# Pairwise feature tower on one core: sums after every eight units, ScalarE copying two units of a run, transposes by halves of rows

## What is computed

```python
e = stack([tbl_f[ids[:, f]] for f in range(32)], axis=1)      # 1024 x 32 x 64
p, q = e[:, ROW], e[:, COL]                                   # 496 pairs
kp = einsum('bpj,ipj->bpi', p, kernel)
z = sum(kp * q, axis=-1)                                      # 1024 x 496
h = concatenate([z, dense_ctx], axis=1)                       # 512 columns
h = maximum(h @ W_top1 + b_top1, 0.0)                         # 512
h = maximum(h @ W_top2 + b_top2, 0.0)                         # 256
y = h @ W_top3                                                # 1024 x 1
```

## Time and profile before

| | |
|---|---|
| median of three executions | 438.9 us |
| the profiled execution | 438.72 us |
| its span | 436.9 us |
| TensorE busy | 429.6 us (98%) |
| VectorE busy | 300.4 us (69%) |
| GpSimd busy | 232.2 us (53%) |
| ScalarE busy | 70.9 us (16%) |
| products, 1984 instructions | 236.2 us |
| sums, 1984 instructions | 120.4 us |
| full transposes, 122 instructions | 26.9 us |

### The profile page before, as it was taken

How to read it: one execution, slowest core, us unless ns; L and a number is a source line. 1 busy time by engine, 2 the same in 40 slices (tenths; PEclk the granted TensorE clock), 3 DMA queues, 4 the chain that set the end, 5 groups by cost and what they waited for, 6 DMA issues and landing times.

```text
span 436.9 us, 10124 instructions
## 1 busy us (share of the span) xinstructions
PE 429.6 (98%) x4308; PEld 286.3 (66%) x4308; DVE 300.4 (69%) x300; ACT 70.9 (16%) x154; POOL 232.2 (53%) x249
## 2 busy tenths in 40 slices
PE   8969999999999999999999999999999999999997
PEld 6646666777677766676677766666667777754442
DVE  4746778877787777877877777887887778860000
ACT  1212110111121101012211110112111010101121
POOL 4777777777776666666466666664666600000000
PEclk9969999999999999999999999999999999999999
DMA  8543454441111111111111111111151100000000
GB/s 242 177 129 85 128 176 131 124 110 29 41 42 25 35 23 26 26 34 23 31 36 23 36 24 23 38 24 28 32 176 38 23 8 14 2 1 1 0 1 0
DMA packets 16513, 23.62 MB, mean 54 GB/s; under 512 B 5778, under 2 KB 9618, under 8 KB 16340
## 3 DMA queue, kind: packets, MB, share of 16 engines
q1 hardware_dynamic: 8080, 14.72, 10.9%
q0 software_dynamic: 7808, 8.01, 9.3%
q10 hardware_dynamic: 580, 0.23, 0.2%
HBM read 20.85 MB, written 0.00 MB: 48 GB/s over the span
## 4 chain that ended last, share of the span: by engine, by line
PE 97%; DMA 1%; POOL 1%; issue 0%; ACT 0%; POOLq 0%
PE kp L594 52%; PE z_ps L611 27%; PE kp L632 6%; PE tr_ps L578 5%; PE kp L638 3%; PE tr_ps L568 2%; PE kp L553 1%; DMA raw<-in_tbl,ids_sb 1%; PE z_ps L568 1%; POOL raw L421 1%; PE kp L645 0%; ACT prod L483 0%; POOL z_sb L411 0%; POOLq L724 0%
## 5 line engine op out<-in xcount | busy, mean ns | idle before, releaser
L531 DVE TENSOR_TENSOR prod<-kp,pair 128x1024 f32<-128x1024 f32 x224 | 260.1, 1217 | 83.4 <-PE kp L594 83.4
L421 POOL DMA_INDIRECT raw<-in_tbl,ids_sb x244 | 231.6, 949 | 117.9 <-issue 62.0
L594 PE MATMUL kp<-pair,k_sb 64*128 64x256 f32 x1984 | 236.2, 387 | 0.0
L594 PEld LDWEIGHTS kp<-pair,k_sb 64*128 64x128 f32 x1984 | 186.1, 188 | 35.7 <-DVE prod L531 6.8
L611 PE MATMUL z_ps<-prod,ones_sel 128*32 128x256 f32 x1984 | 120.4, 382 | 0.0
L611 PEld LDWEIGHTS z_ps<-prod,ones_sel 128*32 128x32 f32 x1984 | 57.9, 110 | 53.6 <-DVE prod L531 14.6
L439 ACT ACTIVATE pair<-tr_ps 128x256 f32<-128x256 f32 x63 | 24.3, 385 | 235.1 <-PE tr_ps L578 225.4
L578 PEld LDWEIGHTS tr_ps<-ident,raw 128*128 128x128 f32 x122 | 12.4, 141 | 27.8 <-issue 27.8
L541 DVE TENSOR_TENSOR prod<-kp,pair 128x512 f32<-128x512 f32 x48 | 30.0, 681 | 0.5 <-PE kp L594 0.5
L578 PE MATMUL tr_ps<-ident,raw 128*128 128x128 f32 x122 | 26.9, 302 | 3.4 <-DMA raw<-in_tbl,ids_sb 3.4
L632 PE MATMUL kp<-z_sb,k_sb 128*128 128x512 f32 x64 | 28.0, 595 | 0.0
(11 more groups left out here) (15 smaller groups left out, 20.2 us busy)
## 6 DMA issues: line engine op xcount, KB each, us to landing
k_sb<-in_kd SPq DMA_DIRECT2D x14, 512.0 KB, 3.8
raw<-in_tbl,ids_sb POOLq DMA_INDIRECT x244
pair<-pair SPq DMA_DIRECT2D x32, 64.0 KB
k_sb<-in_small SPq DMA_DIRECT2D x6, 256.0 KB, 6.6
k_sb<-in_w SPq DMA_DIRECT2D x1, 1024.0 KB
hot_ids_sb<-in_hot_ids SPq DMA_DIRECT2D x3, 256.0 KB, 6.2
k_sb<-in_kd SPq DMA_DIRECT2D x3, 256.0 KB, 2.9
z_sb<-in_dense SPq DMA_DIRECT2D x1, 512.0 KB, 3.6
```

What stands on the lines that cost most here:

```text
L421: nc.gpsimd.indirect_dma_start(raw[:, r % RAW_RING, i, n, :], None, tables[f], bass.IndirectOffsetOnAxis(ap=ids_sb[:, 2 * b + i, f:f + 1], ...
L531: nc.vector.tensor_tensor(prod[:, u % PROD_RING, :, :].rearrange("p q (i n) -> p (q i) n", i=UNIT_SLOTS), kp[u % KP_RING][:, :, :].rearran ...
L594: last = nc.tensor.matmul(kp[u % KP_RING][:, q, i * WIDTH:(i + 1) * WIDTH], k_sb[rows, x, :], pair[rows, group_place(st, owner // 2), :], ...
```

## The change

- Sums are made in batches of eight units from the second stage on (the last batch of a stage has six), and are issued after the seventh unit of the next batch. The first stage keeps batches of four. The run of products between two sums has so many units: seven, then fours, three; from unit 62 on seven, then eights, and sevens at the stage boundaries.
- `z_ps` is 128 x 2 x 256 and a sum takes 512 columns, both slots of a unit at once. The features' places in `z_sb`, the rows of W_top1 and the dense rows follow; the dense load is two planes, of 1 MB.
- In each run from unit 62 on, the units at places 1 and 3 (counted from 0) are copied by ScalarE from `kp` to `prod` (`spill`), and VectorE multiplies them in place in `prod` behind the other units of the run. `DONE_AT` gives each unit's place in VectorE's order. `prod` has 15 places.
- From group 6 of the second stage on an event carries two groups. An event whose unit follows sums is transposed by halves: each 128x128 block as two transposes of 64 rows against a 64x64 identity, into two banks of a `kp` buffer, and ScalarE copies them back in order. Other events keep the full form.
- `raw` has four places, and a gather waits for the event that read its place; the second group of a double event waits for six units more.

```diff
-KP_RING = 3
-PROD_RING = 12
-LAG = 3
-RAW_RING = 8
-RAW_LEAD = 5
+KP_RING = 3
+PROD_RING = 15
+RAW_RING = 4
-STAGES = (1, 1, 1, 1)
+STAGES = ((1,) * GROUPS, (1,) * 6 + (2,) * 5, (2,) * 8, (2,) * 8)
-BATCH_UNITS = (4, 4, 4, 4)
+BATCH_UNITS = (8,) * 4
+FIRST_BATCH_UNITS = (4,) * 8
+SPILL_AT = (1, 3)
+PACE = 6
-CHUNK_UNITS = CHUNK_TILES // (2 * UNIT_SLOTS)
+CHUNK_UNITS = P // 4
...
 def summed_behind(b):
     st, first, n = BATCHES[b + 1]
-    return first + min(LAG, n) - 1
+    return first + (n - 2 if n % 4 == 0 else n - 1)
+
+def spilled_units():
+    return [run[i] for run in runs()[1:-1] for i in SPILL_AT if i + KP_RING < len(run)]
+
+DVE_ORDER = [u for run in runs() for u in [u for u in run if u not in SPILLED] + [u for u in run if u in SPILLED]]
+DONE_AT = {u: i + 1 for i, u in enumerate(DVE_ORDER)}
+
+def done_through(n):
+    return max(DONE_AT[u] for u in range(n))
...
-TRANSPOSE_AT = [0, 0, 0, 1, 2, 4, 7, 10, 13, 16, 19, 23, 27, 31, 35, 39, 43, 47, 51, 55, 59, 61, 65, 69, 73, 77, 81,
-                85, 89, 93, 97, 101, 105, 109, 113, 117, 121, 123, 127, 131, 135, 139, 143, 147, 151, 155, 159, 163,
-                167, 171, 175, 179, 183, 185, 189, 193, 197, 201, 205, 209, 213, 217, 221, 225]
+TRANSPOSE_AT = [0, 0, 0, 1, 2, 4, 7, 10, 13, 16, 19, 23, 27, 31, 35, 39, 43, 47, 51, 55, 59, 62, 65, 69, 77, 85, 93,
+                101, 109, 117, 124, 131, 139, 147, 155, 163, 171, 179, 186, 193, 201, 209, 217]
...
+def gather_unit(r):
+    if r < RAW_RING:
+        return 0
+    e = EVENT_OF[r - RAW_RING]
+    st, k, n, raws = EVENT[e]
+    return TRANSPOSE_AT[e] + PACE if n == 2 and r - RAW_RING == raws[1] else 0
+
+def sums_before(u):
+    return u > 0 and BATCH_OF[u - 1] > 0 and u - 1 == summed_behind(BATCH_OF[u - 1] - 1)
+
+def by_halves(e):
+    return len(EVENT[e][3]) > 0 and sums_before(TRANSPOSE_AT[e])
+
+def home_unit(e):
+    return TRANSPOSE_AT[e] + EVENT[e][2]
...
 # gathers
-                if RELEASE[r]:
-                    pool.wait_ge(transposed, RELEASE[r] + 1)
+                if r >= RAW_RING and EVENT_OF[r - RAW_RING] != (EVENT_OF[r - RAW_RING - 1] if r > RAW_RING else None):
+                    pool.wait_ge(transposed, EVENT_OF[r - RAW_RING] + 1)
+                if gather_unit(r):
+                    pool.wait_ge(kp_done, gather_unit(r))
...
 # ScalarE, behind the evacuations and mixing copies of unit u
+            def spill(u):
+                act.wait_ge(reduced, BATCH_OF[u - PROD_RING] + 1)
+                act.wait_ge(kp_done, u + 1)
+                nc.scalar.activation(prod[:, u % PROD_RING, :, :], kp[u % KP_RING][:, :, :],
+                                     ACT.Copy).then_inc(spilled, 1)
...
 # VectorE
-            for u in range(UNITS):
+            for u in DVE_ORDER:
...
+                if u in SPILLED:
+                    dve.wait_ge(spilled, SPILLED.index(u) + 1)
+                    columns = prod[:, u % PROD_RING, :, :]
+                else:
+                    dve.wait_ge(kp_done, u + 1)
+                    columns = kp[u % KP_RING]
...
 # TensorE, transposes
+                if by_halves(e):
+                    pe.wait_ge(prod_done, DONE_AT[home_unit(e) - KP_RING])
...
+                        rows = raw[:, r % RAW_RING, i, :, :].rearrange("p a n -> p (a n)")
+                        if by_halves(e):
+                            to = ((g - k) * 2 + i) * 64
+                            for h in range(2):
+                                half = slice(64 * h, 64 * h + 64)
+                                last = nc.tensor.transpose(halves_ps(e)[:, h, to:to + 64], rows[half, :],
+                                                           ident[half, half])
...
 # TensorE, products
-                if u >= KP_RING:
-                    pe.wait_ge(prod_done, u - KP_RING + 1)
+                if u - KP_RING in SPILLED:
+                    pe.wait_ge(spilled, SPILLED.index(u - KP_RING) + 1)
+                elif u >= KP_RING:
+                    pe.wait_ge(prod_done, DONE_AT[u - KP_RING])
+                for e in range(len(EVENT)):
+                    if by_halves(e) and home_unit(e) == u:
+                        pe.wait_ge(evacuated, e + 1)
...
 # TensorE, sums
-                for t, u, i, q in tiles:
-                    g = t % 4
-                    col = 2 * ((t % CHUNK_TILES) // 4)
-                    last = nc.tensor.matmul(z_ps[32 * g:32 * g + 32, :], ones_sel[:, 30 - col:62 - col],
-                                            prod[:, u % PROD_RING, q, i * WIDTH:(i + 1) * WIDTH],
...
+                for v, u, q in tiles:
+                    j = v % CHUNK_UNITS
+                    g = 2 * (j % 2) + q
+                    col = 2 * (j // 2)
+                    last = nc.tensor.matmul(z_ps[32 * g:32 * g + 32, :, :].rearrange("p i n -> p (i n)"),
+                                            ones_sel[:, 30 - col:62 - col],
+                                            prod[:, u % PROD_RING, q, :],
```

More of the change, by code:

```diff
@@ L20 @@
 FC = (2 * TILES + DENSE) // P
-CHUNK_TILES = P // 2
+PAIRS = FC // 2
 N1, N2 = HID1 // P, HID2 // P
@@ L142, in batches @@
             first, end = c, min(c + CHUNK_UNITS, SLOTS // UNIT_SLOTS)
-            for n in BATCH_UNITS:
+            for n in BATCH_UNITS if st else FIRST_BATCH_UNITS:
                 out.append((st, unit_at(st, 0) + first, min(n, end - first)))
@@ L156, in batch_tiles, with runs, one_factor @@
     st, first, n = BATCHES[b]
-    return [(2 * s + q, u, i, q) for u in range(first, first + n) for i, s in enumerate(unit_slots(u))
-            for q in range(2)]
+    return [(u - unit_at(st, 0), u, q) for u in range(first, first + n) for q in range(2)]
 def summed_behind(b):
     st, first, n = BATCHES[b + 1]
-    return first + min(LAG, n) - 1
+    return first + (n - 2 if n % 4 == 0 else n - 1)
+def runs():
+    out = [[]]
+    for u in range(UNITS):
+        out[-1].append(u)
+        if BATCH_OF[u] and u == summed_behind(BATCH_OF[u] - 1):
+            out.append([])
+    return out
+def one_factor(u):
+    st = UNIT[u][0]
+    return len({factor_place(st, tile) for x in unit_slots(u) for tile in SLOT[x]}) == 1
+def spilled_units():
+    return [run[i] for run in runs()[1:-1] for i in SPILL_AT if i + KP_RING < len(run)]
+SPILLED = spilled_units()
+DVE_ORDER = [u for run in runs() for u in [u for u in run if u not in SPILLED] + [u for u in run if u in SPILLED]]
+DONE_AT = {u: i + 1 for i, u in enumerate(DVE_ORDER)}
+def done_through(n):
+    return max(DONE_AT[u] for u in range(n))
 def chunk_end(st, c):
-    t = min((c + 1) * CHUNK_TILES, TILES) - 1
-    return BATCH_OF[unit_at(st, t // 2)]
+    return BATCH_OF[unit_at(st, 0) + min((c + 1) * CHUNK_UNITS, SLOTS // UNIT_SLOTS) - 1]
 def mix_unit(st, m):
@@ L183, in mixed_free @@
               if tile[1][1] is not None and mixed_place(*tile[1]) in places]
-    return max(before) + 1 if before else 0
+    return done_through(max(before) + 1) if before else 0
 def gather_order():
     gathers, events = [], []
-    for st, n in enumerate(STAGES):
-        for k in range(0, GROUPS, n):
+    for st, sizes in enumerate(STAGES):
+        for k, n in zip([sum(sizes[:i]) for i in range(len(sizes))], sizes):
             first = len(gathers)
@@ L249, in feature_place, with dense_place @@
 def feature_place(t, n):
[L251 to L256, removed]
-    return 32 * (n // (32 - used)) + used + n % (32 - used)
+    v, i, q = t // 4, t // 2 % 2, t % 2
+    c, j = divmod(v, CHUNK_UNITS)
+    return 2 * c + i, 32 * (2 * (j % 2) + q) + 2 * (j // 2) + n
+def dense_place(n):
+    used = SLOTS // UNIT_SLOTS - (PAIRS - 1) * CHUNK_UNITS
+    i, m = divmod(n, DENSE // 2)
+    return i, 32 * (m // (32 - used)) + used + m % (32 - used)
 def pairwise_tower(nc, dense, ids, hot_ids, row_no, small, tables, kd, ident_in, sel_in, w1, b1, w2, b2, w3, out):
@@ L627, in mlp_step @@
                     for c in range(FC):
-                        if c < FC - 1:
-                            pe.wait_ge(z_out, (after - 1) * (FC - 1) + c + 1)
+                        if c < FC - 2:
+                            pe.wait_ge(z_out, (after - 1) * (PAIRS - 1) + c // 2 + 1)
                         else:
@@ L697 @@
     dense = _np.asarray(inputs["dense_ctx"])
-    dense_rows = _np.zeros((P, BATCH), dense.dtype)
+    dense_rows = _np.zeros((P, 2, BATCH), dense.dtype)
     for n in range(DENSE):
-        w1_rows[FC - 1, dense_row(n)] = pairs + n
-        dense_rows[dense_row(n)] = dense[:, n]
+        i, row = dense_place(n)
+        w1_rows[FC - 2 + i, row] = pairs + n
+        dense_rows[row, i] = dense[:, n]
     kt = _np.concatenate([kin.transpose(2, 1, 0), kin], axis=1)
```

76 lines of the change are left out of this document (43 added, 33 removed).

## The result

The changed kernel takes 422.73 us (median of four, 422.19 to 423.06) beside 438.57 for the kernel before: ratio 0.964, 95% interval 0.962 to 0.966. A second set later gave 423.79 beside 438.65, ratio 0.966 (0.964 to 0.968). Forecast were 422.1 us and a range of 417.5 to 432.0.

A forecast was written before the change was run, and what follows sets the result against it. TensorE, busy for 98% of the span, was taken to bound the kernel. Gains of 8.2, 10.8 and 0.5 (19.5 us) less 2.9 of new waits give 16.6, so 438.7 becomes 422.1 us, range 417.5 to 432.

The forecast's parts named there:

- (a): TensorE's switches between products and sums: 48 periods become 24, each one gone saves 0.34 us, 8.2 us in all.
- (b): Sums of 512 columns: the same columns stream, so at most 0.6 us is saved over 248 units; taken as 0.
- (c): TensorE's transposes: half-form events at 0.33 us double, 0.21 single, and fewer cut runs save 10.8 us (0.6 to 12.3).
- The rule weighed against it: Trainium skill's spacing of weight load and matmul pairs, 0.081 us per half transpose: double event 0.70, 7.4 us worse in all.
- rival 1: Transposes by halves gain nothing, a double event taking 0.74 us and a single one 0.37: 432.4 us, chance 14%.
- (d): GpSimd's gathers: with four places later ones cost nothing; a double event's 10 us is covered by a run of 11.
- Rival 4: TensorE's half clock at 25 to 31.7 us goes too: 1.4 us better, 420.7; chance 60% together with the forecast.
- (e): ScalarE's copies, 1.01 us each, let eight units pass three buffers; products never wait, each wait having 0.22 us to spare.
- rival 2: ScalarE's copy is as slow as Relu, or VectorE's handshakes eat the 0.22 us spare: 424.8 or 427 us, chance 16%.
- (f): TensorE's new waits for VectorE: 1.3 us before unit 69, 1.0 next run, 0.3 each at units 131 and 193; 2.9 together.
- Rival 3: VectorE's multiplication of copied units, both operands in SBUF, waits on GpSimd's gather issues: 20 us, 442 us, chance 5% in full.

The follow-up runs named there:

- the 256-column form: Changed kernel with sums of 256 columns instead of 512, twice as many instructions, part of the sums missing from its result: 425.12 us, ratio 0.970.
- the factor in PSUM: Changed kernel, but from unit 69 on ScalarE also copies each copied unit's factor into PSUM, where VectorE's multiplication reads it: 419.98 us, ratio 0.957.

## Why the prediction was right

The time was right to 0.6 us, and the range held, but errors of opposite sign are in it: the transposes gave 2.7 more and the first stage 1.5 more than forecast, the new waits cost 2.9 more and the late first product 0.6. That they cancel so nearly is luck.

- **(a) Switches, 8.2 us: right.** Products of eight units after full transposes take 7.11 in the chain (7.10 forecast), sums 3.57 (3.59).
- **(b) 512 columns, 0: right to within 0.6** by the trace of the 256-column form; its time left 0.7 to 1.8 more unexplained.
- **(c) Transposes, 10.8: too small, 13.5.** A double event is 0.39, not 0.33, but the products behind it are shorter, 6.97 instead of 7.11; why was not looked into. Net 0.25 and, for one group, 0.27 - 0.14 = 0.13 (0.33 and 0.21 forecast). 20 x (0.74 - 0.25) + 13 x (0.37 - 0.13) + 0.55 = 13.5. The rule weighed against it (0.70 for a double event) and rival 1 fall: eight half instructions take 0.39 with their switch. The recorded text misreads there: the second full transpose stands 0.165 behind the first, as step (c) itself works out, and 0.11 is only its streaming part.
- **(d) Gathers.** In the profiled execution the half clock went (granted 1.00 over the span; 0.992 in the three other executions, which took 422.19 to 423.06) and the stretch to unit 19 came 2.0 earlier, the cap of 1.9 plus a single event by halves; the first product came 0.57 later. Rival 4 is therefore half right. But the sentences that the later gathers "cost nothing" and are "covered" are **the step that failed**, in two ways. First, even in the kernel before GpSimd issues without a rest up to 132.9 us, which the rows of the prediction did not show, so it could not get further ahead, and unit 69 now needs 92 issues where it needed 84, 5.2 us earlier: a wait of 1.89, before any issue is long. Second, a steady run is 10.9 us and its eight issues 10.0, and I held the two against each other without the issues' lengthening (0.9) and without the short runs at the boundaries (10.1 and 9.2 us). The sum of 10.0 and 0.9 leaves nothing over in a long run, so what is lost at a boundary is not made up: the waits of 0.44 and 2.35, which go when the lengthening goes (the factor in PSUM).
- **(e) Copies: right.** ScalarE's 128x1024 copy takes 1.02 (1.01 taken), no product waits inside a steady run; rival 2 falls.
- **(f) New waits, 2.9: all waits from unit 62 on are 5.8.** VectorE's at unit 69 was 0.93 (1.3 forecast); those behind add_dense were hidden by the gather waits and come out at 0.43 to 0.54, or 0.16 to 0.89, when these go (0.3 and 1.0 forecast).
- **Rival 3 had the right pair and the wrong loser.** I let VectorE wait; GpSimd does. Its price was 2.8 to 3.8 us of time (by the factor in PSUM), not 20, for only GpSimd's lateness at units 131 and 201 reaches TensorE.

Sum: 8.2 + 13.5 + 2.0 - 0.2 (the single event counted twice) - 0.6 - 5.8 = 17.1, against 16.4 measured by the spans; the window from unit 124 to 185 agrees with its parts to 0.1 (62 units at 0.863 + 0.431, eight switches of 0.34, eight events of 0.25: 85.0 against 85.06 busy); added up in the same way, the other two windows are 0.4 short of their busy time.

## What to carry to other kernels

When a change makes the bounding engine's period shorter, hold every other engine's work for a period against the new length, with its longest form and over the shortest period, not against the mean: here 10.0 in 10.9 looked covered and was not. And a copy that frees a PSUM buffer moves an operand into SBUF; look at what GpSimd does in the meantime. Before counting on an engine's pauses, look whether it has any where the change will ask more of it: here it had none for the first 130 us.

## What the runs showed of the hardware

- A gather issue that starts 0.06 to 1.0 us into a VectorE multiplication with two SBUF operands is held until it ends, and is done 0.81 to 0.83 us after that: 46 issues in three traces, up to 1.97 us instead of 0.94. One that starts with the multiplication (0.02 behind at most) or before it takes 0.94 or 0.95. VectorE's instruction takes 1.21 to 1.28 either way. With one operand from PSUM, or with no copied unit at all, issues behind the first 40 us take 0.94 to 0.96.
- Four gather issues, one group of 256 rows, take GpSimd 5.0 us (0.94 + 0.30 each); the transposes could start 2.5 us after the start of the last one (120.80 to 123.32).
- Transposes of 64 rows and 64 columns in the array form of the products cost 0.39 us for eight and 0.27 for four, sums before and products behind, and save 0.14 in these products; four full ones cost 0.59.
- A wait of TensorE for a gather can cost more than its length: behind one of 2.26 the next eight units' products took 8.81 instead of 7.13, at a granted clock of 0.64 in the first 4 us; behind one of 2.35 in another execution they took 7.13.
